# Feed-forward of a decoder layer: the last quarter of its activations is scaled and split in rows and turned by a transposing DMA

## The reference

```python
def _L0_ffn_ref(x, W_fc, ln_w, ln_b, W_proj):
    ...
    h = jnp.einsum('btd,hd->bth', x, absmean(W_fc))
    h = jax.nn.gelu(h, approximate=False)
    h = layernorm(h, ln_w, ln_b)
    return jnp.einsum('bth,dh->btd', h, absmean(W_proj))
...
x = x + _L0_ffn_ref(_layernorm(x, axis=-1), L0_ffn_W_fc, L0_ffn_ln_w, L0_ffn_ln_b, L0_ffn_W_proj)
```

## Time and profile before

| | us |
|---|---|
| median of 3 runs | 2554.49 (2551.3 to 2555.81) |
| the profiled execution: its time | 2553.16 |
| its span from first to last instruction | 2551.4 |
| PE busy in the span | 2195.3 (86%) |
| DVE, ACT, POOL busy | 2035.5, 1604.9, 1028.5 |

### The profile page before, as it was taken

How to read it: one execution, slowest core, us unless ns; L and a number is a source line. 1 busy time by engine, 2 the same in 40 slices (tenths; PEclk the granted TensorE clock), 3 DMA queues, 4 the chain that set the end, 5 groups by cost and what they waited for, 6 DMA issues and landing times.

```text
span 2551.4 us, 70786 instructions
## 1 busy us (share of the span) xinstructions
PE 2195.3 (86%) x29031; PEld 1445.0 (57%) x29031; DVE 2035.5 (80%) x4025; ACT 1604.9 (63%) x2354; POOL 1028.5 (40%) x719
## 2 busy tenths in 40 slices
PE   3668889888888888889888888889865899999999
PEld 1435555555555555555555555555533677777776
DVE  6558888888888888888888888888753688888887
ACT  2356666666666666666666666666532777878876
POOL 2133433443344344434433443343221455555553
PEclk7889999999999999999999999999987999999999
DMA  5266777667677666677766667677431233333332
GB/s 137 46 121 112 127 130 121 123 118 128 118 124 129 122 118 123 122 126 124 124 126 118 118 123 130 120 126 126 80 67 46 67 99 91 82 99 90 82 99 59
DMA packets 450784, 277.01 MB, mean 109 GB/s; under 512 B 299344, under 2 KB 401104, under 8 KB 450512
## 3 DMA queue, kind: packets, MB, share of 16 engines
q1 hardware_dynamic: 447408, 272.77, 56.8%
q10 hardware_dynamic: 3104, 0.34, 0.1%
HBM read 54.87 MB, written 33.55 MB: 35 GB/s over the span
## 4 chain that ended last, share of the span: by engine, by line
SPq 44%; PE 32%; DMA 10%; DVE 6%; issue 4%; ACT 3%; POOL 1%; DVEq 0%; ACTq 0%; POOLq 0%
SPq L593 37%; PE ybk L1355 9%; PE hbk L1379 8%; SPq L599 5%; DMA cross_stk<-cross_negmT 5%; PE tbk L1369 4%; PE product_bank L1024 4%; DMA self_stk<-self_negmT 4%; SPq L643 1%; PE score_bank L946 1%; PE score_bank L966 1%; PE exp_bank L946 1%; PE exp_bank L984 1%; DVE cross_mx L828 1%; PE product_bank L1031 1%
## 5 line engine op out<-in xcount | busy, mean ns | idle before, releaser
L730 ACT ACTIVATE prob<-exp_bank 128x1024 f32<-128x1024 f32 x512 | 523.0, 1021 | 288.2 <-PE exp_bank L984 283.8
L828 DVE TENSOR_REDUCE cross_mx<-score_bank 128x8 f32<-128x1024 f32 x256 | 311.2, 1216 | 138.4 <-PE score_bank L966 138.2
L662 POOL TENSOR_TENSOR xs<-xn,xs 128x1024 f16<-128x1024 f32 x64 | 136.2, 2128 | 686.7 <-ACT xs L757 686.7
L828 DVE TENSOR_REDUCE self_mx<-score_bank 128x8 f32<-128x1024 f32 x256 | 310.3, 1212 | 112.2 <-PE score_bank L966 112.2
L662 POOL TENSOR_TENSOR ahl<-attT,ahl 128x512 f16<-128x512 f32 x128 | 148.0, 1156 | 349.5 <-ACT ahl L735 349.4
L1379 PE MATMUL hbk<-wfcT,ffn_xhl 128*128 128x512 f16 x1024 | 262.2, 379 | 6.4 <-ACT hid L1276 3.6
L1339 DVE SCALAR_TENSOR_TENSOR ghl<-tbk,lnwc,ghl 128x512 f16<-128x512 f32 x256 | 188.0, 735 | 98.1 <-ACT ghl L1270 98.0
L1355 PE MATMUL ybk<-wpT,ghl 128*128 128x256 f16 x2048 | 260.5, 273 | 0.8 <-DVE ffn_y L1324 0.7
L1355 PEld LDWEIGHTS ybk<-wpT,ghl 128*128 128x128 f16 x2048 | 197.9, 98 | 66.0 <-DVE ghl L1339 0.9
L946 PE MATMUL exp_bank<-maskBT,pick 64*128 64x512 bf16 x1024 | 155.4, 382 | 74.6 <-ACT prob L730 35.4
L1270 ACT ACTIVATE ghl<-tbk,lnwc 128x512 f16<-128x512 f32 x256 | 174.0, 681 | 67.7 <-PE tbk L1369 67.7
(11 more groups left out here) (159 smaller groups left out, 4642.6 us busy)
## 6 DMA issues: line engine op xcount, KB each, us to landing
self_stk<-self_qk SPq DMA_DIRECT2D x768, 64.0 KB, 2.4
cross_stk<-cross_qk SPq DMA_DIRECT2D x768, 64.0 KB, 2.4
self_src<-in_x SPq DMA_DIRECT2D x32, 512.0 KB, 5.7
ctx_in<-in_ctx SPq DMA_DIRECT2D x32, 512.0 KB, 6.3
x_scratch<-xn SPq DMA_DIRECT2D x32, 512.0 KB, 5.5
ffn_src<-x_scratch SPq DMA_DIRECT2D x32, 512.0 KB, 3.8
out<-ffn_y SPq DMA_DIRECT2D x32, 512.0 KB, 3.6
self_stk<-self_negmT SPq DMA_DIRECT2D x64, 128.0 KB, 3.9
```

Source lines behind the costliest of these rows:

```text
L662: nc.gpsimd.tensor_tensor(out, src, hi, ALU.subtract).then_inc(lo_ready, 1)
L730: act.activation(prob[:, p % 3], ebank[:, :, :], ACT.Exp, scale=EXP_SCALE).then_inc(b.exp_done, 1)
L828: dve.tensor_reduce(a.mx[:, 8 * m:8 * m + 8].rearrange("p (j r) -> p r j", r=2), sbank[:, :, :].rearrange("p r (j k) -> p r j k", j=4), AX ...
```

## The change

Slices 6 and 7 of the hidden width (columns 768 to 1023) no longer go through PE transposes. Instead:

- POOL multiplies these columns of `hid` in place by a copy of the layer-norm weight that lies on all partitions (`scale`, two sequences at a time, so twice a group: once at the end of round k, once in round k + 1 ahead of xs-low). It also computes `hmr` (mean times reciprocal deviation), which DVE did with a minus sign as `hnmr`; base becomes a subtraction.
- ACT rounds the scaled columns to float16 (`rows` high part, 1024 values a partition, here rows-high) behind gelu2; DVE subtracts for the low part (rows-low) in its step 3.
- SP issues one more transposing DMA a round, of `rows` into `gd`, ahead of the one for the normalized input.
- T6, T7, ghi6, ghi7, glo6, glo7 fall away. y6 of a group joins y7 behind T0 of the following round, and y6 waits for the new DMA.

```diff
+    TURNED = 6
+    BY_DMA = FT - TURNED
+    ROWS = TURNED * P
...
+                if here(k - 1):
+                    sp.wait_ge(rows_lo, k)
+                    wait(sp, y_mm, 8 * (k - 1))
+                    sp.dma_start(gd[:, :, :, :, :].rearrange("p a t b s -> p (a t b) s"), rows[:, :, :, :, :].rearrange("p a t b c -> p (a t b c)"),
+                                 transpose=True).then_inc(rows_turned, 16)
                 if here(n):
                     sp.wait_ge(xlo_ready, n + 1)
...
+            def scale(k, half, pair):
+                if isinstance(k, int) and k == 0 and pair == 0:
+                    pool.wait_ge(rows_in, 16)
+                pool.wait_ge(hstats_done, 8 * k + 4 * pair + 4)
+                some = hid[:, half, 2 * pair:2 * pair + 2, ROWS:]
+                pool.tensor_tensor(some, some, lnw_rows[:, :].unsqueeze(1).broadcast_to([P, 2, F - ROWS]), ALU.mult).then_inc(scaled, 1)
...
+                    pool.wait_ge(hrstd_ready, q + 1)
+                    wait(pool, shift_ready, q)
+                    pool.tensor_tensor(hmr[:, :], hmv[:, 1 - half, :, 0], hrstd[:, 1 - half], ALU.mult).then_inc(hmr_ready, 1)
+                    scale(q, 1 - half, 1)
...
+                if here(k):
+                    scale(k, half, 0)
...
-                    if here(q):
-                        act.wait_ge(gT_ready, 8 * q + s + 1)
+                    if here(q) and s < TURNED:
+                        act.wait_ge(gT_ready, TURNED * q + s + 1)
...
+                    if s == 2 and here(q):
+                        act.wait_ge(scaled, 2 * q + 2)
+                        wait(act, rows_turned, 16 * q)
+                        act.activation(rows[:, HI], hidden_rows(1 - half), ACT.Copy).then_inc(rows_hi, 1)
...
-                    if s == 2 and here(q):
-                        dve.wait_ge(hrstd_ready, q + 1)
-                        wait(dve, shift_ready, q)
-                        dve.scalar_tensor_tensor(hnmr[:, :], hmv[:, 1 - half, :, 0], -1.0, hrstd[:, 1 - half], ALU.mult, ALU.mult).then_inc(hnmr_ready, 1)
...
+                    if s == 3 and here(q):
+                        dve.wait_ge(rows_hi, q + 1)
+                        dve.tensor_tensor(rows[:, LO], hidden_rows(1 - half), rows[:, HI], ALU.subtract).then_inc(rows_lo, 1)
...
                     if s == 0 and here(f):
+                        second(f, FT - 2)
                         second(f, FT - 1)
...
-                        for t in ((), (), (0,), (1,), (2,), (3,), (4,), (5, 6))[s]:
+                        for t in ((), (), (0,), (1,), (2,), (3,), (4,), (5,))[s]:
                             second(q, t)
```

More of the change, by code:

```diff
@@ L107, in decoder_layer_kernel @@
         att = attention(nc, stack, ins, sh, x2_dram, prep)
-        mlp = ffn(nc, stack, sh, x2_dram, out, att)
+        mlp = ffn(nc, stack, ins, sh, x2_dram, out, att)
         LAST = 2 * (NG + 4)
@@ L1147, in attention, with ffn @@
         return part
-def ffn(nc, program, sh, x2_dram, out, before):
+def ffn(nc, program, ins, sh, x2_dram, out, before):
     x2_groups = x2_dram.rearrange("(n b) s d -> n s b d", b=G)
@@ L1177, in ffn @@
         hrstd = sb("hrstd", [P, 2, G])
-        hnmr = sb("hnmr", [P, G])
-        ghl = sb("ghl", [P, 2, FT, T], F16)
+        hmr = sb("hmr", [P, G])
+        ghl = sb("ghl", [P, 2, TURNED, T], F16)
         y = sb("ffn_y", [P, 2, G, D])
+        rows = sb("g_rows", [P, 2, BY_DMA, G, S], F16)
+        gd = sb("g_turned_rows", [P, 2, BY_DMA, G, S], F16)
+        lnw_rows = sb("ffn_lnw_rows", [P, F - ROWS])
         held = sb("ffn_held_wait", [P, 2, G + 1])
@@ L1192, in ffn @@
         h_mm, hid_ready, hstats_done, hmv_ready = sem("h_mm"), sem("hid_ready"), sem("hstats_done"), sem("hmv_ready")
[L1193 removed]
+        hve_ready, hrstd_ready, hmr_ready = sem("hve_ready"), sem("hrstd_ready"), sem("hmr_ready")
         gT_ready, ghi_ready, glo_ready = sem("gT_ready"), sem("ghi_ready"), sem("glo_ready")
+        rows_in = sem("ffn_rows_in")
+        scaled, rows_hi, rows_lo, rows_turned = sem("g_scaled"), sem("g_rows_hi"), sem("g_rows_lo"), sem("g_rows_turned")
         shift_ready, base_ready = sem("shift_ready"), sem("base_ready")
@@ L1250, in pool_body @@
                     pool.wait_ge(xc_ready, q + 1)
-                    pool.tensor_tensor(y[:, 1 - half], y[:, 1 - half], xc[:, 1 - half], ALU.add).then_inc(base_ready, 1)
+                    pool.tensor_tensor(y[:, 1 - half], xc[:, 1 - half], y[:, 1 - half], ALU.subtract).then_inc(base_ready, 1)
                 if here(n):
@@ L1256, in pool_body, with hidden_rows @@
                                        ALU.add).then_inc(xc_ready, 1)
+                if here(k):
+                    scale(k, half, 0)
+        def hidden_rows(half):
+            return hid[:, half, :, ROWS:].rearrange("p b (t c) -> p t b c", t=BY_DMA)
         def act_body(i):
@@ L1288, in act_body @@
                     if s == 3 and here(q):
-                        act.wait_ge(hnmr_ready, q + 1)
+                        act.wait_ge(hmr_ready, q + 1)
                         wait(act, stored[1 - half], 16 * (q // 2) if isinstance(q, int) else 16 * (i - 1 + half))
                         for b in range(G):
-                            last = act.activation(y[:, 1 - half, b], sh.s2B[:, :], ACT.Copy, scale=hnmr[:, b:b + 1])
+                            last = act.activation(y[:, 1 - half, b], sh.s2B[:, :], ACT.Copy, scale=hmr[:, b:b + 1])
                         last.then_inc(shift_ready, 1)
@@ L1349, in second @@
             def second(q, t):
-                pe.wait_ge(glo_ready, 8 * q + t + 1)
+                if t < TURNED:
+                    pe.wait_ge(glo_ready, TURNED * q + t + 1)
+                elif t == TURNED:
+                    pe.wait_ge(rows_turned, 16 * (q + 1))
                 for b in range(G):
@@ L1354, in second @@
                     for part in (HI, LO):
-                        last = pe.matmul(ybk[:, b], ghl[:, part, t, b * S:(b + 1) * S], sh.wpT[:, t],
+                        turned = ghl[:, part, t, b * S:(b + 1) * S] if t < TURNED else gd[:, part, t - TURNED, b, :]
+                        last = pe.matmul(ybk[:, b], turned, sh.wpT[:, t],
                                          start=(t == 0 and part == HI and b % 2 == 0), stop=(t == FT - 1 and part == LO),
@@ L1363, in pe_body @@
                 for s in range(STEPS):
-                    if here(q):
+                    if here(q) and s < TURNED:
                         if s == 0:
                             pe.wait_ge(hid_ready, 8 * (q + 1))
-                        wait(pe, glo_ready, 8 * q + s - (2 if s > 2 else (5 if s == 2 else 1)))
+                        wait(pe, glo_ready, TURNED * q + s - 2)
                         for b in range(G):
```

10 lines of the change are left out of this document (6 added, 4 removed).

## The result

| | us |
|---|---|
| before, median of 7 runs | 2553.86 (2548.52 to 2555.81) |
| after, median of 7 runs | 2564.11 (2559.73 to 2571.95) |
| ratio after to before, 95% interval | 1.0055 (1.0036 to 1.0074) |
| profiled executions, span | 2551.4, then 2570.1 |

A forecast was written before the change was run, and what follows sets the result against it. PE's list alone was taken to bound the kernel (round 17.43). After the change POOL's loop sets 18.0, 0.57 more over 29 rounds (+16.5); together +15.5 on 2554.5 gives 2570, range 2553 to 2590.

The forecast's parts named there:

- h6 waits for gelu4: On PE at h6: ACT's stretch with rows-high makes gelu4 late, so PE waits 1.29 us a round.
- The loop of ACT and PE: T0 through h2, gelu2, rows-high, gelu4, h6 to the next T0: a round of 17.84 us, 0.88 saved and 1.29 lost.
- POOL's loop: From rows-high through xs-high, xs-low, base, xc and both multiplications back to rows-high: 17.99 us, setting a round of 18.0.
- The sign that the forecast gave for a POOL loop that sets the round: If POOL's idle time before `ffn_ve` (2.46) remains, its loop isn't closed: the round is 17.84, the time 2565.
- Rival 3: It cancels: rows-high at 0.6 and the multiplication near 1.0 put both loops at 17.45, time 2554; chance 0.13.
- What stays hidden: Rows-low on DVE (1.2) and the new DMA (landing 4.3 later, 3.0 of slack before y6) delay nothing.
- rival 5: DVE 0.8 us later makes rows-low delay xs-low by up to 1.2 a round: +50, 2604; chance 0.05.
- the rule on the shared port pair: A two-SBUF-input DVE instruction and a GpSimd instruction reading SBUF exclude one another for a whole instruction; forecast to add nothing.
- rival 2: ACT's stretch from gelu2 to h6 is 7.18, so h6 doesn't wait: 2528 in full; chance 0.10 for under 2549.
- The tail: In the last rounds, the turned rows arrive about when PE finishes y5: about nothing, 1 either way.

The follow-up runs named there:

- rows-high early: Changed kernel with ACT's rows-high moved behind ghi0 and POOL's second multiplication moved to the head of its round; ratio to before 1.0010.
- the run with all three moves: Changed kernel with rows-high behind ghi0 (second multiplication heading POOL's round), xc in POOL's idle time before xs-low, ACT's shift behind gelu4; ratio to before 0.9924.
- shift behind gelu4 alone: Changed kernel with only ACT's four shift rows moved from ahead of ghi4 to behind gelu4; round 18.43 in the loop, 18.02 written out.

## Why the prediction was right

- **h6 waits for gelu4: right.** Place, instruction and number: one wait a round, 1.24 by starts where 1.29 was forecast. Rows-high cost 0.94, forecast 0.96. Rows-high done twice moved the round by its whole length; moved ahead of gelu0, together with the second multiplication, it took 0.43 off.
- **The loop of ACT and PE: 17.84 forecast, 17.71 written out, 17.92 in the loop.** The terms, by written-out rounds, are T0 to h2 4.81 (4.78), gelu2 1.06 behind (1.06), gelu2 to gelu4 7.73 (7.82), to h6 0.63 (0.65), to the next T0 3.48 (3.46 by its four parts; the forecast added PE's wait to 16.55, which is 0.07 more than those parts make). I took all rounds to be alike; that 26 of them run in a loop which costs 0.2 each once nothing hides it was not in the sum. The two misses, 0.13 too much and 0.21 too little, nearly cancel: luck.
- **"So POOL's loop is a little longer than the loop of ACT and PE, and the round is 18.0": wrong.** The step that failed was the sum of POOL's loop, 17.99. In the round of the loop shown POOL has 0.22 left at rows-high's start, about 0.05 of that the hand-over, so its loop is 17.70. The multiplication itself is 1.27, just as priced; the distances around it were too long: 1.23 rather than 1.27 between starts, 2.31 rather than 2.36 for xc, 1.09 rather than 1.18 from `hrstd` to `hmr` (in every second round it is 1.18), 0.15 rather than 0.22 for `hmr`, 4.17 rather than 4.21 to xs-high. In the written-out rounds, where one multiplication more found 0.26, the loop is 17.45: `ffn_ve` to `hrstd` is 1.54 there, priced 1.72, and rows-high to xs-high 4.09. Left out, the second multiplication gained 0.05. The sign that the forecast gave for a POOL loop that sets the round, no idle time before `ffn_ve`, doesn't tell: that time is gone, and the slack is ahead of rows-high. The 2570 rests on this loop; the other gave 2565.5, and the measured median is 2564.1. As the two lie so near, the wrong one gave nearly the right time, and that too is luck.
- **Rival 3 is priced by one loop only.** By its own terms the loop of ACT and PE would be 17.48, but POOL's 17.99 - 0.36 - 2 x 0.27 = 17.09, not 17.45. The longer one sets the round, so its 2554 stays about as it is.
- **What stays hidden: right.** The DMA lands in 4.3, y6 never waits in the steady rounds; rows-low takes 1.215, priced 1.2.
- **Rows-low holding up xs-low (rival 5):** not seen. In the round shown xs-low starts at 2188.32, 1.14 behind xs-high's start, as before; rows-low runs from 2186.31 while POOL is idle. The pair of engines did meet elsewhere, with another instruction of DVE that has two SBUF inputs: `ffn_nmr` stood until POOL's instruction ended, 2.30 rather than 0.17 beside xc, and 0.5 to 1.0 beside a multiplication (six times with rows-high twice, ten times with one multiplication more). That agrees with the rule on the shared port pair that the prediction takes from the Trainium skill ("SBUF — State Buffer"). Beside the four-value `hrstd`, by the same rule also excluded for its whole length, the trace differs: with rows-high early, `ffn_nmr` ran from 2173.04 for 0.15 while `hrstd` ran from 2172.41 to 2173.42. Rows-low itself met POOL only in the last round of the changed kernel. Base started 0.25 before its end there and took 2.46 rather than 2.36, so what a full overlap with xs-low would cost stays untried.
- **PE's saving kept (rival 2):** not in this kernel, but its condition, a stretch short enough that h6 doesn't wait, was met in the run with all three moves. Its round of 16.55 came out as 16.63 there, and as 16.55 without the loop.
- **The tail, "about nothing":** 0.8 shorter.

## What to carry to other kernels

Busy shares do not tell which engine is next: ACT had 20% idle time, and its stretch between two hand-overs was full to 0.07 us. Before taking work from the engine that sets the time, follow the other engines' starts between what they receive and what they give back, and put new work where its engine stands idle (here behind ghi0), not where its data first exists. And when two loops through one instruction are within 0.3 us of each other, cut both in one edit: one alone gained 0.4 of 1.3 us here, or lost.

## What was not expected of the hardware

- PE's granted clock held 1.00 in the steady rounds with one wait of 1.1 us a round (changed kernel), and with two of 0.7 (shift behind gelu4 alone). With one of 2.0 a round (rows-high twice) it fell to 0.96 in half of the 40 us stretches: six of 24 rounds then lose 1.56 us behind the wait.
- A loop on the engines costs little while PE is always busy (0.03 a round before, 0.08 in the fastest version) and 0.2 a round where it waits for ACT, by kernels with and without the loop. Against the last three rounds only, it is up to 0.4 with the shift alone.
- A DVE instruction of 0.15 us with two inputs in SBUF can take as long as the POOL instruction beside it: 2.30 beside xc. Moving work on POOL can so lengthen a path on DVE and ACT that doesn't wait for that work.
